# First mixture of experts: 39 routed tiles of 128 slots in full fp32 become 23 pairs of 256 slots in three short-form passes

## What is computed

```
X = X + ctx @ wo
h2 = rmsnorm(X, norm2_w).reshape(B * S, d)
probs = softmax(h2 @ router_w)
topw, topi = top_k(probs, 2);  topw = softmax(topw)
combine = sum(one_hot(topi, 8) * topw[..., None], axis=1)
shared = (silu(h2 @ sh_gate) * (h2 @ sh_up)) @ sh_down
eout[e] = (silu(h2 @ e_gate[e]) * (h2 @ e_up[e])) @ e_down[e]   # 256 -> 512 -> 256, for each expert
moe_out = shared + sum_e(eout[e] * combine[:, e])
return X + moe_out
```

## Time and profile before

| what | us |
|---|---|
| median of 3 runs (1434.55 to 1436.48) | 1434.56 |
| the profiled execution | 1429.93 |
| its span | 1428.1 |
| PE busy / DVE busy / ACT busy / POOL busy | 1273.5 / 853.7 / 570.3 / 638.7 |

### The profile page before, as it was taken

One profiled execution on the slowest core, in us unless ns is written; L12 is line 12 of the kernel. 1 busy time (PEld: TensorE's weight loads), 2 busy tenths in 40 slices (PEclk: granted clock), 3 DMA queues, 4 the chain that ended last, 5 costly groups with the idle time before them and its releaser, 6 DMA issues.

```text
span 1428.1 us, 35852 instructions
## 1 busy us (share of the span) xinstructions
PE 1273.5 (89%) x13189; PEld 1066.0 (75%) x13189; DVE 853.7 (60%) x2071; ACT 570.3 (40%) x1272; POOL 638.7 (45%) x885
## 2 busy tenths in 40 slices
PE   5999879989999999989999999689989999549895
PEld 4777658977777788768989999667767887448674
DVE  4888833348888788757311121379866788744335
ACT  2555545424444555633222222135444555314220
POOL 4455531036664455620233333268764444355253
PEclk9999989989999999999999999899999999869997
DMA  6000000020000000001699999510000000069933
GB/s 258 3 2 0 2 31 1 1 93 17 16 12 2 9 17 11 20 9 45 228 327 317 344 333 325 186 54 27 8 13 20 24 30 17 18 199 356 278 101 111
DMA packets 47376, 137.88 MB, mean 97 GB/s; under 512 B 6925, under 2 KB 29646, under 8 KB 41104
## 3 DMA queue, kind: packets, MB, share of 16 engines
q1 hardware_dynamic: 32944, 110.37, 22.0%
q0 software_dynamic: 7536, 19.67, 4.4%
q10 hardware_dynamic: 6768, 6.16, 1.3%
HBM read 119.54 MB, written 17.56 MB: 96 GB/s over the span
## 4 chain that ended last, share of the span: by engine, by line
PE 55%; DVE 22%; issue 9%; POOL 5%; DMA 5%; ACT 2%; DVEq 0%; SPq 0%; POOLq 0%; ACTq 0%
PE ps L1118 10%; PE ps L1352 10%; PE ps L1036 7%; DVE negmax L1794 6%; PE ps L1364 5%; PE ps L1080 4%; PE ps L1060 3%; PE ps L981 3%; DMA row_in<-rows_of,from_u 3%; PE ps L984 2%; PE ps L922 2%; PE ps L1087 2%; DVE u L1760 2%; PE ps L969 1%; POOL gn L887 1%
## 5 line engine op out<-in xcount | busy, mean ns | idle before, releaser
L1418 ACT ACTIVATE probsT_all<-ps 128x1024 f32<-128x1024 f32 x128 | 131.1, 1024 | 165.1 <-PE ps L984 165.1
L1794 DVE TENSOR_REDUCE negmax<-ps 128x8 f32<-128x1024 f32 x128 | 156.0, 1218 | 45.7 <-PE ps L981 45.3
L1352 PE MATMUL ps<-hT,w_tile 128*128 128x128 f32 x1304 | 164.6, 281 | 10.7 <-issue 5.3
L1352 PEld LDWEIGHTS ps<-hT,w_tile 128*128 128x128 f32 x1304 | 156.6, 197 | 14.0 <-issue 13.2
L984 PE MATMUL ps<-qe,kf 32*128 32x256 f32 x1280 | 151.4, 384 | 0.0
L981 PE MATMUL ps<-kf,qe 32*128 32x128 f32 x2048 | 146.8, 282 | 0.0
L981 PEld LDWEIGHTS ps<-kf,qe 32*128 32x128 f32 x2048 | 128.2, 188 | 1.6 <-issue 0.8
L758 POOL TENSOR_SCALAR eps_sum<-mv 128x1 f32<-128x1 f32 x112 | 25.4, 227 | 220.5 <-DVE mv L1731 131.0
L984 PEld LDWEIGHTS ps<-qe,kf 32*128 32x128 f32 x1280 | 109.5, 187 | 3.9 <-issue 2.7
L2356 DVE TENSOR_TENSOR h_in<-ps,act_sb 128x512 f32<-128x512 f32 x39 | 27.0, 692 | 140.0 <-PE ps L1352 126.5
L1411 ACT ACTIVATE hT<-ps,vecs 128x128 f32<-128x128 f32 x142 | 47.1, 385 | 143.7 <-PE ps L1337 118.6
(11 more groups left out here) (287 smaller groups left out, 3232.0 us busy)
## 6 DMA issues: line engine op xcount, KB each, us to landing
w_tile<-in_w_f SPq DMA_DIRECT2D x29, 1536.0 KB
w_tile<-in_w_f SPq DMA_DIRECT2D x47, 385.0 KB
y_back<-in_w_f SPq DMA_DIRECT2D x10, 1536.0 KB
back_of<-w_odd ACTq DMA_DIRECT2D x47, 128.0 KB
ctxT<-in_ctxT SPq DMA_DIRECT2D x32, 128.0 KB, 2.0
rows_of<-nv SPq DMA_DIRECT2D x32, 128.0 KB, 1.7
w_even<-in_w_att SPq DMA_DIRECT2D x3, 1024.0 KB, 7.0
y_back<-back_of SPq DMA_DIRECT2D x6, 512.0 KB, 5.4
```

The lines of the kernel that those rows point to most:

```text
L1352: last = mm(ps[:, 2 * which + at.two, fc * P:(fc + 1) * P], w[:, col:col + P], rowT[:, at.two, c, :], start=c == 0, stop=c == KC - 1)
L1418: nc.scalar.activation(half_of(probsT_all, half), ps[:, 2:4].rearrange("p b n -> p (b n)"), ACT.Exp, scale=HD ** -0.5).then_inc(S["probs"], 1)
L1794: nc.vector.tensor_reduce(m, ps[:, 0:2].rearrange("p b (h k) -> p (b h) k", h=HB), AX.X, ALU.max, negate=True).then_inc(S["s_max"], 1)
```

## The change

MOE0's routed work is cut in pairs of 256 slots of one expert instead of tiles of 128. Each expert's slots are rounded up to 256, which makes N_PAIRS = (4096 + 8 x 255) // 256 = 23 pairs, or 46 tiles. The tables of `slots` and `origins` grow from 39 to 46 columns. For each pair:

- PE: four transposes, 48 products for gate and up (hi x hi, hi x lo, lo x hi; 256 moving columns) in two halves, 24 for the second product. Order in a step k: turn(k+1), up(k, half 0), up(k, half 1), down(k-1).
- ACT and DVE split the loaded fp32 weights on chip, in three pieces of 1024 columns, and the rows and the hidden values too. ACT now copies the result out as well (`pair_result`), 512 columns at once.
- SP: three buffers for the loaded weights; buffer j % 3 is free again when DVE has made the low part of pair j-3's last piece.
- POOL: two indirect fetches for each pair, four pairs ahead, and two indirect sends.

The decay table of RET (1 MB) leaves `const`, since its place is needed; SP loads it in the middle of the pairs, behind RET's weights. The first two pieces of pair 0's weights are split at the end of the dense part. MOE1 keeps its tiles; only its counts of semaphores change.

```diff
+N_PAIRS = (2 * NT * P + 8 * (2 * P - 1)) // (2 * P)
+RAW_BUFS = 3
+ROW_PAIRS = 4
# SP
+            def load_pairs():
+                for j in range(N_PAIRS):
+                    b = j % RAW_BUFS
...
+                    else:
+                        sp.wait_ge(S["down_lo"], j - RAW_BUFS + 1)
+                    sp.dma_start(raw[b][:, 0:keep], A["w_f%d" % MOE0][bass.ds(e + 1, 1)]...)
+                    if j == N_PAIRS // 2:
                         load_attention(RET)
+                        sp.wait_ge(S["t_up"], 2)
+                        sp.dma_start(decay_sb[:], A["const"][:, C_DECAY:C_COLS]).then_inc(S["decay_in"], 16)
# POOL
+            def move_pairs():
...
+                for j in range(ROW_PAIRS):
+                    fetch_pair(j)
+                for j in range(N_PAIRS):
+                    if j + ROW_PAIRS < N_PAIRS:
+                        fetch_pair(j + ROW_PAIRS)
+                    if j:
+                        send_pair(j - 1)
+                send_pair(N_PAIRS - 1)
# PE
+            def pair_up(at, part):
+                if part == 0:
+                    pe.wait_ge(S["up_lo"], at.j * 2 + 2)
+                    pe.wait_ge(S["pair_lo_sb"], at.j + 1)
...
+            def pair_down(at):
+                pe.wait_ge(S["t_lo"], at.j * 2 + 2)
+                pe.wait_ge(S["down_lo"], at.j + 1)
...
# ACT
+            def split_high(tile, piece_):
...
+                copy(hi[:, cols], raw[j % RAW_BUFS][:, cols]).then_inc(S["up_hi" if piece_ < 2 else "down_hi"], 1)
+            def pair_hidden(j, part):
...
+                nc.scalar.activation(act_sb[:, part], ps[:, part, :], ACT.Silu).then_inc(S["t_act"], 1)
+                act.wait_ge(S["t_h"], q + 1)
+                copy(t_hi[:, j % 2, part * 2 * D:(part + 1) * 2 * D], h_in[:, part]).then_inc(S["t_hi"], 1)
+            def pairs_of_tiles():
+                pair_high(0)
+                for j in range(N_PAIRS):
+                    if more:
+                        pair_high(j + 1)
+                    if j >= 2:
+                        pair_result(j - 2)
+                    if more:
+                        split_high(Pair(0, j + 1), 0)
+                    pair_hidden(j, 0)
+                    if more:
+                        split_high(Pair(0, j + 1), 1)
+                    pair_hidden(j, 1)
+                    split_high(Pair(0, j), 2)
+                pair_result(N_PAIRS - 2)
+                pair_result(N_PAIRS - 1)
# DVE
+            def split_low(tile, piece_):
+                tt(dst[:, cols], raw[j % RAW_BUFS][:, cols], hi[:, cols].bitcast(f32), ALU.subtract)...
+            def pair_low(j):
+                for c in range(KC):
+                    last = stt(out=pair_lo[j % 2][:, c], in0=ps[:, 6 + j % 2, c * D:(c + 1) * D], scalar=vec("n2_w", c), ...)
+            def pair_hidden(j, part):
+                tt(h_in[:, part], ps[:, 2 + part, :], act_sb[:, part], ALU.mult).then_inc(S["t_h"], 1)
+                dve.wait_ge(S["t_hi"], q + 1)
+                tt(t_lo[:, j % 2, cols], h_in[:, part], t_hi[:, j % 2, cols].bitcast(f32), ALU.subtract).then_inc(S["t_lo"], 1)
+            def pairs_of_tiles():
+                pair_low(0)
+                for j in range(N_PAIRS):
+                    if more:
+                        split_low(Pair(0, j + 1), 0)
+                    pair_hidden(j, 0)
+                    if more:
+                        pair_low(j + 1)
+                        split_low(Pair(0, j + 1), 1)
+                    pair_hidden(j, 1)
+                    split_low(Pair(0, j), 2)
```

More of the change, by code:

```diff
@@ L474, in w_uses, with of_tiles @@
[L474 to L483, removed]
+        def of_tiles(name, n):
+            return n + N_PAIRS * (2 if name in ("t_gate", "t_up", "t_act", "t_h") else 1)
@@ L576, in load @@
+                    e = sp.value_load(expert_of[j:j + 1, 0:1], min_val=0, max_val=F_ROUTED[MOE0] - 1)
+                    sp.dma_start(raw[b][:, 0:keep], A["w_f%d" % MOE0][bass.ds(e + 1, 1)].rearrange("a p n -> (a p) n")
                                  ).then_inc(S["w_tile_in%d" % b], 16)
[L578 to L581, removed]
+                    if j == N_PAIRS // 2:
@@ new lines, in pair_up @@
+            def pair_up(at, part):
+                hi, lo, _ = pair_weights(at)
+                if part == 0:
+                    pe.wait_ge(S["up_lo"], at.j * 2 + 2)
+                    pe.wait_ge(S["pair_lo_sb"], at.j + 1)
+                for which, name, free in ((0, "t_gate", "t_act"), (1, "t_up", "t_h")):
+                    if not at.first:
+                        pe.wait_ge(S[free], at.j * 2 + (part - 1))
+                    for i in range(2):
+                        for c in range(KC):
+                            col = (which * KC + c) * 4 * P + (2 * part + i) * P
+                            wh, wl, xh, xl = hi[:, col:col + P], lo[:, col:col + P], pair_hi[at.two][:, c], pair_lo[at.two][:, c]
+                            last = three(ps[:, 2 * which + part, i * D:(i + 1) * D], ((wh, xh), (wh, xl), (wl, xh)), c == 0, c == KC - 1)
+                    last.then_inc(S[name], 1)
@@ new lines, in pairs_of_tiles, with step @@
+            def pairs_of_tiles():
+                def step(i, k):
+                    whole = not isinstance(i, int)
+                    first = not whole and k == 0
+                    if first:
+                        pair_up(Pair(i, k), 0)
+                    if whole or k + 1 < N_PAIRS:
+                        pair_turn(Pair(i, k + 1))
+                    if whole or k < N_PAIRS:
+                        if not first:
+                            pair_up(Pair(i, k), 0)
+                        pair_up(Pair(i, k), 1)
+                    if whole or k:
+                        pair_down(Pair(i, k - 1))
+                pair_turn(Pair(0, 0))
+                for k in range(3):
+                    step(0, k)
+                rounds_ = (N_PAIRS - 4) // ROW_PAIRS
+                with pe.Fori(0, rounds_) as i:
+                    for k in range(3, 3 + ROW_PAIRS):
+                        step(i, k)
+                for k in range(3 + ROW_PAIRS * rounds_, N_PAIRS + 1):
+                    step(0, k)
@@ L1784, in decay @@
                 first = strips(half, True)[0]
-                by_head = const[:, C_DECAY:C_COLS].rearrange("p (c j n) -> p j c n", c=KC, j=4)[:, first:first + 2]
+                if half == 0 and tile.t == 0:
+                    dve.wait_ge(S["decay_in"], 16)
+                by_head = decay_sb[:].rearrange("p (c j n) -> p j c n", c=KC, j=4)[:, first:first + 2]
                 bank = first_key_bank(tile, half)
```

404 lines of the change are left out of this document (250 added, 154 removed).

## The result

| | before | after |
|---|---|---|
| median, us | 1434.55 (5 runs, 1430.8 to 1436.5) | 1444.81 (5 runs, 1440.3 to 1450.9) |
| profiled execution / its span | 1429.9 / 1428.1 | 1443.5 / 1441.7 |

The medians differ by 10.3 us, a ratio of 1.0072; the ratio on record is 1.009 with a 95% interval of 1.0061 to 1.0119. The change makes the kernel slower by 10 us; 9.1 were forecast. Beside later experiments the changed kernel ran on two more chips, with ratios of 1.0051 (1.0026 to 1.0076) and 1.0064 (1.0043 to 1.0085), thus +7.6 and +9.0 us.

A forecast was written before the change was run, and what follows sets the result against it. ACT's and DVE's circle of hand-overs, 9.7 us for each of the pairs, was taken as the bound. Last result +7.8 and end +1.3 made +9.1 on 1434.6: 1443.7 us, forecast 1439 to 1450, stated range 1436 to 1460.

The forecast's parts named there:

- The ring: Routed stage: hand-overs between ACT and DVE form a circle from pair to pair, 9.7 us each, 0.8 above PE's work.
- four steps: Alternating parts of the circle in one pair: ACT 3.89 us, DVE 1.86, ACT 0.66, DVE 3.27.
- PH: ACT's two row copies of 256 columns with the gain, from PSUM: 0.85 us full, 0.80 to the next start.
- PE's need: PE's work for each pair, 72 products and four transposes: 8.91 us.
- The first rival: PE stays the bound in the routed stage at 8.91 us for each pair: 17 us less, 1427; chance 0.10.
- The margin of the weights: Loads of 1536 KB take at most 7.2 us, hidden by 1.7; RET's 2 MB cost 0 to 3, taken as 0.
- The start: Before the steady pairs: larger tables +0.5 us, first product at 695.8 instead of 694.2, ACT's iteration 0 at 699.1.
- The last rival: PE's clock falls to 1.2 GHz in each pair's 0.8 us gap; at mean 0.9, 9.9 a pair, 1448 us; chance 0.05.
- The end: Behind the last result: same chain of send, landing and load, with one more POOL issue, +1.3 us.
- No overlap of neighbours: ACT's and DVE's instructions take full durations, 10.5 us for each pair: +17, 1461; chance 0.08.
- Weights late in every pair: Loads of 11.0 us make each pair wait up to 2 us, up to 1486; 9.5 gives 1457; chance 0.08.
- DVE blocked by POOL: DVE's subtractions with two SBUF inputs wait for POOL's issues, 0.6 us for each pair: +13, 1457; chance 0.06.

The follow-up runs named there:

- x_in_ring: Changed kernel plus one more ACT copy of 1024 columns before the split of the next pair's first weight part, in 20 pairs; 1440.5 us against 1421.8 unedited.
- x_in_gap: Changed kernel plus one more ACT copy of 1024 columns between half 0's silu and its hidden copy, where ACT idles; 1420.3 us against 1421.8 unedited.
- rows_gap_x: Changed kernel with ACT's row and result copies moved before the first hidden copy, plus an extra 1024-column copy before the next pair's first split; 1435.5 us, period 9.285.
- reorder: Changed kernel with ACT's row copies, result copy and down-weight split moved into its two idle gaps; 1406.8 us against 1421.8 unedited, period 8.99.
- again: The changed kernel unedited, run once more on chip B; 1421.8 us, period 9.545.
- ret_last_again: Changed kernel with ACT's copies and split in its gaps, pair 1's second weight piece split earlier, RET's loads behind the last pair's weights; 1425.8 us against 1441.7.
- reorder_first: Changed kernel with ACT's copies and split in its gaps, and pair 1's second weight piece split before iteration 0's first hidden values; 1425.9 us, chip C.
- turn_first: Changed kernel with PE transposing pair 1's rows before pair 0's first products; 1442.2 us against 1441.7.
- pl_in_gap: Changed kernel with DVE's two row operations of the next pair moved to its wait before the first low part; 1434.6 us against 1441.7, period 9.11.

## Why the prediction was right, and where it was off

**The ring** held. It was put at 9.7 and measured at 9.545. By its four steps, from the starts above and with the hand-overs counted as in the prediction: ACT's part 3.89 forecast, 3.78 measured (PH took 0.71 and not 0.80, R 0.48 and not 0.52); DVE's SL and H 1.86 and 1.86; C 0.66 and 0.67; DVE's L, PL, SL, H 3.27 and 3.24. Most of the 0.15 is PH (0.09), the term whose nearest row had another source. Over 20 pairs it is 3.1 us less. x_in_ring, x_in_gap and rows_gap_x show that it is a ring and that this is its length.

**PE's need** was put at 8.91 and is 8.99 in reorder. The first rival's time, 1427, was 7.6 us under the kernel before; reorder is 7.4 under it (1406.8 against 1414.2). This is the comparison with the prediction's 15 us less a longer start and end. That reorder is also 15 us under the changed kernel is another difference.

**The margin of the weights** was put at 1.7 us, from a load of at most 7.2; in again the loads take 6.6 to 7.9 us, median 7.3. Steady pairs don't wait in the ring; at 8.99 for each pair they do, as reorder shows. I took RET's 2 MB as free; they cost 0.5 us. The range of 0 to 3 held it, and rows_gap_x's 1.87 too.

**The start** was mis-sized most. ACT's iteration 0 was to begin at 699.6 (with the tables) and began at 704.90. Of the 5.3 us, 0.75 is drift from earlier stages. The tables themselves cost 0.55 against 0.5. Then 0.1 until the rows are there, and 0.5 in the turn, PH and PL (2.7 us from the turn to the first product, 2.2 forecast). The clock took 1.4: PE stood idle from the end of the dense part to 697.75 but for four transposes, and then the granted clock was 0.57 on average until 701, that is mostly at the 1.2 GHz level, so that 24 products took 4.2 us and not 2.8 (windows view; columns as above):

```profile
697.00:701.00 4.00, 3.25 (x16) 3.28 (x17) 0.61 (x2) 0.00 (x0) 2.92 (x4) 0.57 0.96 357
...
711.00:717.00 6.00, 5.09 (x24) 5.09 (x25) 4.59 (x5) 3.73 (x6) 0.00 (x0) 0.50 0.00 0
```

The same happens once more at 711, after PE waited 6.0 us for DVE's split of pair 1's weights (705.9 to 711.9). The last rival spoke of such a clock in every pair; it was there only at the start, and in the steady part the clock is 1.00. The length of the gap alone does not tell: behind the gap before pair 1's first product the clock stayed at 1.00 in rows_gap_x (3.2 us) and ret_last_again (1.9 us), and fell in reorder_first (1.8 us). The first three microseconds behind it, rows_gap_x and then reorder_first:

```profile
709.00:712.00 3.00, 3.00 (x25) 3.00 (x26) 2.04 (x3) 2.44 (x4) 0.00 (x0) 1.00 0.13 26
```

```profile
707.00:710.00 3.00, 3.00 (x19) 3.00 (x20) 2.30 (x4) 2.56 (x5) 0.00 (x0) 0.67 0.21 44
```

The last 2.5 us of the 5.3 are open. I let ACT go on right behind the second turn. The row of that turn starts at 701.99, which is 7.3 us behind the issue of its last rows (694.67), as late as turn_first's 7.2; yet ACT and POOL, which both wait for this turn, go on only at 704.90 and 705.14, and on chip B ACT goes on at once.

**The end**: the last iteration took 11.3 us (915.17 to 926.45) against 10.8. From the start of the last result copy to the first use of the results are 7.48 us (925.85 to 933.33), against 6.31 before (914.56 to 920.87): +1.2, forecast +1.3.

**The sum**: start +5.3, iterations 0 to 21 -2.1 (the shorter period, RET's wait and 0.5 more in iteration 1 together), last iteration +0.5, so the last result came 3.6 us later than forecast (926.45 against 922.8). With 0.9 more behind the stage, which no term covers, the single execution is 13.6 us over the one before, not 9.1. The medians of three chips say +10.3, +7.6 and +9.0, so part of this belongs to the two profiled executions (the one before was 4.6 under its median, the one after 1.3), and the start was 2 us shorter on chip B. The forecast's 1443.7 is 1.1 below the median, closer than its steps deserve: periods too long by 3 us together and a start too short by 5 offset each other, and the medians lie 3.3 us closer than the profiled executions. That closeness is luck; the ring and its length are not.

Two slips of the prediction change nothing in its sum. The chain of the earlier trace rows leaves PE four times for a row fetch of about 9 us, not five. And with full durations the ring's own terms give 10.3 and not 10.5 unless hand-overs within an engine are added.

**The rivals.** PE as the bound: refuted by the period, and brought about by reorder. No overlap of neighbours: the starts above overlap by 0.08 to 0.13. Weights late in every pair: no wait in steady pairs. DVE blocked by POOL: POOL's issues stand at 783.18, 784.50, 785.80 and 787.10, beside SL, H, L and SL, three of them begun before the subtraction beside them, and the subtractions keep their time (line view of DVE, 720 to 900 us: min/median/max ns):

```profile
L2548 DVE TENSOR_TENSOR lo_even<-w_tile,hi_even x19: 1212/1224/1228, 720.2 to 892.8; 128x1024 fp32r<-128x1024 f32 x19
```

The other three forms of the split look alike, and none is over 1.228 us. The Trainium skill (SBUF — State Buffer, Who interferes with whom) lets either engine block the other; in this stage SL (at most 1.228 us) and L (at most 0.695, from 720 to 900 us) lost no time to POOL's indirect DMAs. No run here says what other POOL work would do.

## What to carry to other kernels

When work is moved from one bound engine to two idle ones, busy shares say that it fits, and the order says whether it runs: follow the hand-overs from one instruction round to the same instruction of the next item, and compare that ring with the bound engine's need. Then put what has slack into the places where an engine already waits; the same instructions in another order were worth 15 us of 1420 here, and turned a loss of 0.5% into a gain of 0.5% on chip B, and of 0.6% into 0.45% on chip D. After each shortening look for the parallel branch that is next, and for the first item, whose inputs land while the DMA queues are full.

## What the runs showed that I had not expected

- Two branches of a ring can lie within half a microsecond of each other: 0.79 us taken out gave 0.435 of period in pl_in_gap.
- In turn_first the rows of an indirect fetch of 128 rows were used 2.8 us after its issue with DMA at 0.30 (694 to 697), and 7.2 us after it beside a 1536 KB load and further fetches (0.93, 697 to 704).
- Once PE was the bound, ACT waited 15 us for weights in reorder and PE had no gap for it; the time for a load, put at one period in the prediction, shrinks with the period from 9.545 to 8.99.
- The same kernels differ by 20 us between chips (1414 and 1434 for the one before), nearly all of it behind this stage: from the last result copy to the end are 496.0 us in again and 515.9 in after.
